# Where a late expert's up products stand: in front of the second attention's projections instead of behind them

## The reference, cut to what matters

```python
x = x + s * g                      # layer 0: attention, ternary feed-forward
xn = _layernorm(x, axis=-1)
s = _L1_attn_ref(xn, L1_attn_Wq, L1_attn_Wk, L1_attn_Wv, L1_attn_Wo)      # causal, 16 heads of 8
g = _silu(_L1_ffn_ref(xn, L1_ffn_w_gate, L1_ffn_w_up, L1_ffn_w_down))     # inputs rounded to fp4 in blocks of 16
...
h12 = jnp.einsum('btd,ehd->bteh', x, w12)                                 # layer 3: 8 experts, 2 x 256 each
h1, h2 = (h12[..., :H], h12[..., H:])
hidden = jax.nn.silu(h1) * h2
expert_out = jnp.einsum('bteh,edh->bted', hidden, w3)
y = jnp.sum(total_probs[..., None] * expert_out, axis=-2)
```

## Time and profile before

| | us |
|---|---|
| median of 3 runs | 3758.95 (3758.35 to 3760.73) |
| the profiled execution's own time | 3768.15 |
| its span | 3766.1 |
| TensorE busy | 3414.2 (91%) |
| VectorE busy | 2487.1 (66%) |
| ScalarE busy | 1798.1 (48%) |
| GpSimd busy | 977.2 (26%) |

### The profile page before, as it was taken

One profiled execution on the slowest core, in us unless ns is written; L12 is line 12 of the kernel. 1 busy time (PEld: TensorE's weight loads), 2 busy tenths in 40 slices (PEclk: granted clock), 3 DMA queues, 4 the chain that ended last, 5 costly groups with the idle time before them and its releaser, 6 DMA issues. The chain is left out here.

```text
span 3766.1 us, 56142 instructions
## 1 busy us (share of the span) xinstructions
PE 3414.2 (91%) x20181; PEld 1785.1 (47%) x20181; DVE 2487.1 (66%) x5466; ACT 1798.1 (48%) x3832; POOL 977.2 (26%) x845
## 2 busy tenths in 40 slices
PE   7999899989998999988999989989999889999887
PEld 3445534545355544455444553454534554445544
DVE  5576666676566765767656765767656776576676
ACT  3554444544544535545445544445355453554434
POOL 1133311432023410333114330243202341133323
PEclk8999999999999999999999999999999999999998
DMA  5100101102011021000111010110200001100140
GB/s 173 35 18 24 51 23 35 37 4 72 1 35 40 1 72 32 15 29 34 39 35 34 8 66 7 35 40 1 72 19 28 29 28 45 35 16 25 46 111 24
DMA packets 80571, 138.69 MB, mean 37 GB/s; under 512 B 9670, under 2 KB 55910, under 8 KB 77606
## 3 DMA queue, kind: packets, MB, share of 16 engines
q1 hardware_dynamic: 75976, 120.94, 10.1%
q10 hardware_dynamic: 4320, 14.11, 1.2%
HBM read 105.13 MB, written 29.10 MB: 36 GB/s over the span
## 5 line engine op out<-in xcount | busy, mean ns | idle before, releaser
L707 DVE TENSOR_REDUCE nmax<-banks 128x1 f32<-128x512 f32 (+3 forms) x1216 | 760.3, 658 | 337.8 <-PE banks L510 206.7
L627 ACT ACTIVATE probs<-banks 128x512 f32<-128x512 f32 (+3 forms) x1024 | 478.8, 526 | 255.8 <-PE banks L529 148.2
L145 PE MATMUL banks<-filler,identb 128*128 128x512 bf16 x1896 | 495.5, 379 | 9.3 <-PEq L493 9.3
L529 PE MATMUL banks<-qs,ks 74*128 74x512 bf16 (+3 forms) x1536 | 440.7, 328 | 36.2 <-ACT probs L627 13.8
L510 PE MATMUL banks<-ks,qs 72*128 72x512 bf16 (+3 forms) x1536 | 436.9, 329 | 39.0 <-DVE nmax L707 20.2
L510 PEld LDWEIGHTS banks<-ks,qs 72*128 72x128 bf16 x1536 | 140.6, 97 | 312.7 <-DVE nmax L707 162.6
L145 PEld LDWEIGHTS banks<-filler,identb 128*128 128x128 bf16 x1896 | 179.1, 98 | 209.5 <-issue 56.3
L1570 ACT ACTIVATE probs<-banks,nm 128x192 f32<-128x192 f32 x512 | 172.1, 421 | 206.7 <-DVE nm L1522 206.7
L627 ACT ACTIVATE early<-banks 128x256 f32<-128x256 f32 (+3 forms) x512 | 196.5, 438 | 152.4 <-PE banks L529 151.8
L1604 POOL TENSOR_TENSOR probs<-probs,inv 128x768 f32<-128x768 f32 x128 | 187.0, 1466 | 253.6 <-DVE inv L1532 253.6
L529 PEld LDWEIGHTS banks<-qs,ks 74*128 74x128 bf16 x1536 | 141.0, 98 | 222.2 <-ACT probs L627 75.7
(11 more groups left out here) (501 smaller groups left out, 6694.5 us busy)
## 6 DMA issues: line engine op xcount, KB each, us to landing
qs<-parts_scratch SPq DMA_DIRECT2D x300, 96.0 KB
ks<-parts_scratch SPq DMA_DIRECT2D x288, 96.0 KB
parts_scratch<-parts SPq DMA_DIRECT2D x50, 384.0 KB, 2.6
shared<-in_w_h SPq DMA_DIRECT2D x17, 1024.0 KB, 6.8
shared<-in_w SPq DMA_DIRECT2D x26, 256.0 KB, 4.0
layers<-in_layers ACTq DMA_DIRECT2D x1, 3250.0 KB, 24.7
qs<-max_parts SPq DMA_DIRECT2D x192, 4.0 KB
xn<-in_x SPq DMA_DIRECT2D x9, 256.0 KB, 2.8
```

Source lines behind the costliest of these rows:

```text
L145: nc.tensor.matmul(K.ps[:, bank, :], K.identb[:, :], K.filler[:, :], start=True, stop=True)
L529: mm = nc.tensor.matmul(K.ps[:, b, q0:T], K.ks[0:KR, h, k * P:(k + 1) * P], K.qs[0:KR, h, q0:T], start=True, stop=not on_tensor)
L627: nc.scalar.activation(probs[:, 4 * (q % QUADS) + m % 4, q0:T], K.ps[:, bank("second", m), q0:T], ACT.Exp, scale=scale).then_inc(exped, 1)
L707: nc.vector.tensor_reduce(nmax[:, t, h:h + len(heads)], K.ps[:, n % 2, 0:len(heads) * keys].rearrange("p (j k) -> p j k", k=keys), AX.X, A ...
```

## The change

In the prepare block of the second attention:
- TensorE's 13 fillers at the opening go, and the four up products of halves 0 and 1 of the first late expert stand there. Their Silus open the block on ScalarE, and their two multiplies stand on VectorE ahead of the fp4 rounding.
- behind the values' products TensorE no longer does those halves. It turns the fp4 input (once the values have been read, which move from bank 2 to bank 7), projects the gate (once `left` is 2), and does the up products of halves 2 and 3 and the first late expert's down products. Before, the turn and these products stood at the start of the attention's block.
- on ScalarE the Silu of half 2 stands ahead of the second parts of queries and keys, and the Silu of half 3 and the copy of the turned input behind them.

A few steps further on in the opening of the attention change places (`HID`, `ADD`, `GATE_READ`). The third preparation (`rms`) keeps its fillers.

```diff
--- before.py
+++ after.py
@@ -279,7 +279,7 @@
                     beside.run(beside.on_vector, -14)
                 if then:
                     shift[1](dve)
-                v = K.ps[:, 3 if rms else 2, :].rearrange("p (t h d) -> p t h d", t=NT, d=HD)
+                v = K.ps[:, 3 if rms else 7, :].rearrange("p (t h d) -> p t h d", t=NT, d=HD)
                 if not rms:
                     dve.wait_ge(projected, 3)
                     nc.vector.tensor_copy(K.v32[:, :, :, 0:HD], v).then_inc(v_used, 1)
@@ -317,8 +317,10 @@
 
             @block.tensor
             def _(pe):
-                keep_busy(nc, K, 3, 13)
+                if not rms:
+                    beside.run(beside.on_tensor, -29)
                 if rms:
+                    keep_busy(nc, K, 3, 13)
                     for t in range(NT):
                         pe.wait_ge(xr_ready, t + 1)
                         nc.tensor.transpose(K.ps[:, 7, t * P:(t + 1) * P], K.xr[:, t, :],
@@ -335,16 +337,16 @@
                 nc.tensor.matmul(K.ps[:, 4, :], wq[:, :], srcT[:, :], start=True, stop=True).then_inc(projected, 1)
                 nc.tensor.matmul(K.ps[:, 5, :], wk[:, :], srcT[:, :], start=True, stop=True).then_inc(projected, 1)
                 for t in range(NT):
-                    mm = nc.tensor.matmul(K.ps[:, 3 if rms else 2, t * P:(t + 1) * P], srcT[:, t * P:(t + 1) * P],
+                    mm = nc.tensor.matmul(K.ps[:, 3 if rms else 7, t * P:(t + 1) * P], srcT[:, t * P:(t + 1) * P],
                                           wv[:, :], start=True, stop=True)
                 mm.then_inc(projected, 1)
                 if not rms:
 
-                    beside.run(beside.on_tensor, -22)
+                    beside.run(beside.on_tensor, -27)
                     pe.wait_ge(v_used, 1)
-                    beside.run(beside.on_tensor, -21)
+                    beside.run(beside.on_tensor, -26)
                     pe.wait_ge(left, 2)
-                    beside.run(beside.on_tensor, -20)
+                    beside.run(beside.on_tensor, -19)
 
                 def banks_free():
                     pe.wait_ge(v_used, NT)
@@ -368,6 +370,7 @@
                                          scale=K.rmsw_col[:, 0:1]).then_inc(xrT_ready, 1)
                     shift[0](act)
                 else:
+                    beside.run(beside.on_scalar, -29)
                     act.wait_ge(turned, NT)
                     nc.scalar.activation(srcT[:, :], K.ps[:, 6, :], ACT.Identity).then_inc(xnT_ready, 1)
                 for m, b in enumerate((bq, bk)):
@@ -375,7 +378,7 @@
                     nc.scalar.activation(parts[:, m, 0, :], K.ps[:, 4 + m, :], ACT.Identity,
                                          bias=0.0 if b is None else b).then_inc(first, 1)
                 if not rms:
-                    beside.run(beside.on_scalar, -22)
+                    beside.run(beside.on_scalar, -28)
                 for m in range(2):
                     act.wait_ge(left, m + 1)
                     nc.scalar.activation(parts[:, m, 1, :], rest[:, m, :], ACT.Identity).then_inc(first, 1)
@@ -925,11 +928,11 @@
         self.late = range(E3 - len(self.DOWN), E3)
 
 
-    UP = -22, -21, -10, -10, -4.5, -2.5
-    DOWN = -9, -2, 1
-    HID = -9.6, -9.6, -7.5, -5.5, -2.5, -1.5
-    ADD = -2.9, -1.2, 1
-    GATE, GATE_READ, SCORES, DONE = -20, -8.5, -1, 8
+    UP = -30, -29, -28, -27, -4.5, -2.5
+    DOWN = -19, -2, 1
+    HID = -30, -29, -9.6, -9.5, -4, -2.4
+    ADD = -7, -1.2, 1
+    GATE, GATE_READ, SCORES, DONE = -20, -9.7, -1, 8
     GATE_BANK = 4
 
     def tensor(self, pe):
@@ -1241,6 +1244,7 @@
     FILLED = {12: (5, 1), 13: (5, 2), 14: (5, 1)}
     TAIL = 2, 3, 2
     KEEPS_BUSY = False
+    XQ_STEP = -26
     UP_STEPS = -9.4, -5, -3, -1
 
     def __init__(self, nc, K, ctx, early):
```

## The result

| | before | with the change |
|---|---|---|
| median of 6 runs | 3760.82 us (3758.35 to 3764.64) | 3777.66 us (3775.12 to 3780.48) |
| the profiled execution | 3768.15 us | 3780.48 us |
| its span | 3766.1 us | 3778.6 us |

The ratio of the runs is 1.0043, with a 95% interval of 1.0032 to 1.0053: slower by 0.43%, some 17 us, and clear of the 0.2% that the prediction drew as its limit.

What follows compares the result with a forecast made beforehand. TensorE was taken as busiest, with the preparation's path over VectorE and TensorE's after the barrier. Schedule +3 us and clock +8 us gave +11 us: 3770 for the median, range 3758 to 3782.

Steps and rivals of the forecast that it cites:

- Step 7: TensorE quiet 4.2 us before the gate except for turns: four clock falls in eight samples at 2.1 us, +8 us.
- Steps 1 to 6, the schedule: Prepare block and attention's opening: barrier 5.7 us later, 5.3 us saved behind it; +0.4 us a sample, +3 us in all.
- step 1: Block's opening on TensorE: four up products replace 13 fillers; second Silu holds up the turned input's copy by some 0.15 us.
- step 2: VectorE's two multiplies ahead of the fp4 rounding lie on the path: about +0.85 us, bounds 0.5 and 1.3.
- step 3: TensorE behind the rests: gate, four up and eight down products, less about 0.25 us for overlapped ends; 6.65 us.
- Step 6: ScalarE's new order moves stores and loads back by 5.1 us; first scores covered by 6 us.
- The signs: Profile after, from the block's start: rests end near 593.0, barrier some 19.1 us and first scores 30.6 us behind it.
- The third: Rival: a longer clock fall in every sample's preparation, as turns may not count as work; 3779 to 3788, chance 0.14.
- The clock holds: Rival: TensorE's clock holds or falls once or twice; 3762, up to 3766 with two falls; chance 0.28.
- The rival of a gain: Attention's block starts before 599.7, first scores come earlier: -1 to -2 us a sample, 3743 to 3755; chance 0.10.

Runs made afterwards that it cites:

- run with fillers: The change plus 12 fillers behind the values' products and 2 behind the turn of the fp4 input; 3762.43 us, ratio 0.9997 to the kernel before.
- the fourth run: Against the change: up products of halves 2 and 3 in the quiet stretch, the gate's projection behind them, no fillers; 3735.42 us, ratio 0.9932 to the kernel before.
- the run with second parts first: Against the change: ScalarE's Silu of half 2 again behind the second parts of queries and keys; 3778.46 us, ratio 1.0042 to the kernel before.

## Why the prediction was right, and where it was not

I forecast 3770 against 3758.95, slower by 11 us, with the range 3758 to 3782. Measured were 3777.66 against 3760.82, slower by 17. The sign, the mechanism and its place were right. Two terms were mis-sized, in opposite directions: +8 us for the clock where it was some 15, and +3 us for the schedule where it was -1. That the time still lies within the forecast's own 3764 to 3779 is so in part because these errors partly cancelled.

**Step 7, the clock.** The quiet stretch is where I put it: 4.24 us from the values' last product (589.56 + 1.05) to the gate at 594.85, with one turn in it, against 4.2 forecast. The price was right as well: 27.75 - 25.85 = 1.9 us for a sample, against 2.1. The *count* failed. I took four falls in eight samples because the crossing to the next sample had shown two in seven. There were eight. The row that should have moved me was in my own text: the place is quieter than any that I had compared it with (0.64 us of work in 4.20, against 1.51 in 3.50 where it fell and 1.87 in 3.40 where it held). A frequency taken at a place where the clock sometimes falls says little of a much quieter one. Eight times 1.9 is 15.2 us. The run with fillers bears it out: 3777.66 - 3762.43 = 15.2, and 17 us by the ratios, so that the agreement to a tenth is luck. One sentence of step 7 was wrong: that a fall ahead of the gate hurts little and one that comes with it in full. The three early falls cost 2.4 to 2.5 us (28.28 to 28.39 against 25.85), the falls near the gate 1.4 to 1.7.

**Steps 1 to 6, the schedule.** +0.4 us a sample forecast, -0.15 measured with the fillers. The pieces: the copy was not held up by the second Silu (4.20 us behind the statistics, 4.19 before), where step 1 had charged 0.15. The rests began 6.41 us behind the copy, 0.72 later than before, where step 2 had 0.85. From the gate to the attention's block I had 7.0 us and it took 6.70 (605.53 - 598.83): I took too little off for overlapped ends in step 3. From there to the first scores it was 11.40 against 11.5. Step 6 held for the change: the third parts came 6.1 to 7.2 us later than before and no first scores waited for a load. But its cover of 6 us was thinner than I had taken it for: with the fillers the third parts came 4.7 us late, and in one sample of eight a load held the first scores up by 0.7 us.

**The signs.** In sample 2 the rests ended 11.90 us behind the block's start (12.0 forecast). The third parts came 1.1 us, the barrier 1.1 us and the first scores 1.0 us later than forecast (17.55, 20.19 and 31.59 us behind the block's start), as those figures were given without a fall. The copies of following samples lay 444.7 to 448.7 us apart, against about 446.

**The rivals.** The third, a fall in every sample, is what happened, with the chance of 0.14. Its condition (turns don't count) is refuted, and its longer falls came in three samples of eight, so its 3779 to 3788 was too high for the median. "The clock holds" did not come true; with the fillers that time is what one gets, 3762.43 against the 3762 that it named. The rival of a gain needed the attention's block to start before 599.7, 14.5 us behind the copy. With the fillers it starts 14.45 us behind it and the first scores come 0.15 us earlier than before, so the point lies at 14.6 us and was right to within 0.1 us. A version of it that moves up products, not down products, gives the 28 us of the fourth run. I had written that nothing let the products behind the rests start sooner; half of them needed only bank space that was free, and the gate stood in front of them for no other reason than the order in the generator.

What stays open: why the clock stays low twice as long when it falls early. The runs show only that it does so: in the change and in the run with second parts first, all five falls that came 5.7 to 6.0 us behind the copy lasted 6.8 us, and all eleven that came at 6.9 us or later lasted 3.4. Open too is whether the two more falls elsewhere in the loop belong to the change or to where its samples happened to lie. The six further runs had between none and six such falls. With one exception all of them, in all eight traces, stand at the same three places: the crossing to the next sample (96 to 98 us ahead of the copy), 67 to 69 us behind the copy, and 227 to 232 us behind it.

## What to carry to other kernels

Before moving work off a stretch where another engine sets the pace, add up what TensorE has left to do there. If little is left, the work behind it may run at half the clock, as it did here in eight of eight samples, and that cost more (1.9 us a sample) than the moves themselves. Fill such a stretch with products of the path that need nothing from the slower engine (28 us gained here); 14 fillers only restored the old time, and four restored nothing that could be measured.

## What was not expected of the hardware

Four fillers of 1.03 us in a quiet stretch of some 4.2 us changed neither the number of falls (8 of 8) nor the time beyond its noise (3779.53 us), while 12 and 2 held the clock in all samples. Twenty f32 turns of 2.35 us in all held it too. Where the clock fell early in the idle stretch, it stayed low twice as long and cost 2.4 us or more in place of 1.4 to 1.7. And eight falls in eight samples are more than the crossing (two in seven before) had led me to think.
